# Causal attention in one fp32 product of exponentials and values, instead of two fp16 halves

## What is computed

```python
q = (x @ Wq).reshape(B, S, HEADS, HEAD_DIM).transpose(0, 2, 1, 3)
c_kv = x @ Wkv_down
k = (c_kv @ Wk_up)...        # 16 heads of 32
v = (c_kv @ Wv_up)...
# the last 24 columns of each head of q and k are rotated
scores = jnp.einsum('bhqd,bhkd->bhqk', qf, kf) * scale
scores = jnp.where(causal, -jnp.inf, scores)
weights = jax.nn.softmax(scores, axis=-1)
out = jnp.einsum('bhqk,bhkd->bhqd', weights, v)
```

## Time and profile before

| | |
|---|---|
| median of 3 runs | 1692.59 us (1692.43 to 1700.83) |
| the profiled execution | 1692.4 us, span 1690.6 us |
| PE busy | 1443.2 us (85%), granted clock 0.936 of full |
| DVE busy | 1273.0 us (75%) |
| ACT busy | 903.6 us (53%) |
| POOL busy | 846.8 us (50%) |

### The profile page before, as it was taken

One profiled execution on the slowest core, in us unless ns is written; L12 is line 12 of the kernel. 1 busy time (PEld: TensorE's weight loads), 2 busy tenths in 40 slices (PEclk: granted clock), 3 DMA queues, 4 the chain that ended last, 5 costly groups with the idle time before them and its releaser, 6 DMA issues.

```text
span 1690.6 us, 26867 instructions
## 1 busy us (share of the span) xinstructions
PE 1443.2 (85%) x9924; PEld 869.5 (51%) x9924; DVE 1273.0 (75%) x2115; ACT 903.6 (53%) x1431; POOL 846.8 (50%) x724
## 2 busy tenths in 40 slices
PE   4767787776668988848799999999999999999984
PEld 2345545444544444423356655666566655665553
DVE  4849899899867999975957767767766766766757
ACT  3327566565664544445455565556555565556542
POOL 6418385564352123687644654456454654466421
PEclk9969898989779999968999999999999999999997
DMA  9050010000211010110001000100101100100002
GB/s 282 26 200 2 28 51 2 28 26 27 100 51 50 26 70 32 51 63 13 25 26 38 26 26 29 35 26 26 37 26 31 33 26 26 38 26 26 13 1 100
DMA packets 63105, 74.62 MB, mean 44 GB/s; under 512 B 6912, under 2 KB 40320, under 8 KB 61952
## 3 DMA queue, kind: packets, MB, share of 16 engines
q1 hardware_dynamic: 62400, 68.68, 12.1%
q10 hardware_dynamic: 576, 4.19, 0.6%
HBM read 49.66 MB, written 10.49 MB: 36 GB/s over the span
## 4 chain that ended last, share of the span: by engine, by line
PE 60%; DVE 24%; issue 11%; ACT 3%; POOL 2%; DMA 1%; SPq 0%; DVEq 0%; POOLq 0%; ACTq 0%
PE banks L1103 48%; PE banks L870 6%; DVE nmf L1473 5%; DVE plo L1487 2%; PE banks L935 1%; DVE cat L1456 1%; PE banks L923 1%; DVE top L1599 1%; DVE wk L1595 1%; DVE att L1497 1%; DVE kcT L1463 1%; DMA w_fold<-w_top 1%; DVE attf L1606 1%; PE banks L1058 1%; DVE qcT L1483 1%
## 5 line engine op out<-in xcount | busy, mean ns | idle before, releaser
L1103 PE MATMUL banks<-xc,w 128*128 128x512 f16 x2688 | 591.2, 382 | 17.7 <-ACT banks L1144 15.0
L1103 PEld LDWEIGHTS banks<-xc,w 128*128 128x128 f16 x2688 | 264.2, 99 | 339.2 <-ACT banks L1144 20.2
L1103 PE MATMUL banks<-wd,mid 128*128 128x256 f16 x2688 | 298.1, 273 | 5.4 <-ACT banks L1144 3.1
L1103 PEld LDWEIGHTS banks<-wd,mid 128*128 128x128 f16 x2688 | 263.6, 98 | 40.9 <-ACT banks L1144 3.4
L847 POOL TENSOR_TENSOR mid<-m,mid 128x512 f16<-128x512 f32 x64 | 75.1, 1174 | 318.2 <-ACT mid L1144 318.2
L753 POOL TENSOR_TENSOR plo<-pf,phi 128x896 f16<-128x896 f32 x64 | 133.5, 2088 | 175.3 <-ACT phi L1144 175.2
L1144 ACT ACTIVATE banks<-banks 128x512 f32<-128x512 f32 x192 | 108.7, 579 | 193.0 <-PE banks L1103 193.0
L847 POOL TENSOR_TENSOR mid<-msum,mid 128x512 f16<-128x512 f32 x128 | 186.4, 1475 | 2.6 <-ACT mid L1144 2.6
L1421 DVE SCALAR_TENSOR_TENSOR w<-stage,w 128x512 f16<-128x512 f32 (+1 forms) x56 | 61.5, 1138 | 106.0 <-ACT w L1144 106.0
L1144 ACT ACTIVATE mid<-msum 128x512 f16<-128x512 f32 x128 | 81.2, 635 | 84.1 <-DVE msum L1780 28.1
L1473 DVE TENSOR_REDUCE nmf<-banks 128x1 f32<-128x512 f32 (+3 forms) x256 | 107.3, 480 | 14.9 <-PE banks L937 14.4
(11 more groups left out here) (252 smaller groups left out, 2910.8 us busy)
## 6 DMA issues: line engine op xcount, KB each, us to landing
stage<-w_fold SPq DMA_DIRECT2D x24, 256.0 KB, 3.0
stage<-in_Wg SPq DMA_DIRECT2D x24, 256.0 KB, 3.1
stage<-in_Wu SPq DMA_DIRECT2D x24, 256.0 KB, 3.1
stage<-in_Wd SPq DMA_DIRECT2D x24, 256.0 KB, 2.8
vcat<-vnext SPq DMA_DIRECT2D x8, 528.0 KB, 3.2
x_in<-in_x SPq DMA_DIRECT2D x4, 1024.0 KB, 6.3
x_res<-in_x SPq DMA_DIRECT2D x4, 1024.0 KB, 5.6
c_raw<-in_ctx SPq DMA_DIRECT2D x4, 1024.0 KB, 5.6
```

The lines of the kernel that those rows point to most:

```text
L1103: mm = nc.tensor.matmul(out, l(x, i), r(y, i), start=start and i == 0 and j == 0, stop=stop and i == k - 1 and j == 2, skip_group_check=True)
```

## The change

The exponentials stay as ACT writes them, in float32, and are the stationary operand of one fp32 matmul for each block, against 33 columns of float32 values (32 and the ones). `hi` and `lo` are gone on ACT, POOL and DVE, with `phi` and `plo`; `pf` has four buffers (`PB = 4`). `vcat` and `vnext` hold 33 floats instead of 66 halves, so they have the same bytes and ACT alone writes them (`v` on DVE is gone). `osb` has 33 columns for each block of rows, `comb` loses its addition. The raw weights at the start lie in `pf`. The split of `wqw` stands at other places of the last tables. `A_PE` is unchanged.

```diff
 A_ACT = steps("""
-    xT.0 xT.1 exp.0 xT.2 xT.3 exp.1 hi.0 hi.1 row.0 exp.2 c.0 pv.0 hi.2 row.1 rhi.0 exp.3 row.2 rhi.1 pv.1 hi.3
+    xT.0 xT.1 exp.0 xT.2 xT.3 exp.1 row.0 exp.2 c.0 pv.0 row.1 rhi.0 exp.3 row.2 rhi.1 pv.1 
...
-        vcat = sb(sa, "vcat", [P, H, TT, 66], F16)
-        pf = sb(sa, "pf", [P, 2, TRI])
-        phi = sb(sa, "phi", [P, 2, TRI], F16)
-        plo = sb(sa, "plo", [P, 2, TRI], F16)
-        osb = sb(sa, "osb", [P, 2, G, TT, 65])
+        vcat = sb(sa, "vcat", [P, H, TT, HD + 1])
+        pf = sb(sa, "pf", [P, PB, TRI])
+        osb = sb(sa, "osb", [P, 2, G, TT, HD + 1])
...
                     elif k == "pv":
 
-                        pe.wait_ge(p_lo_pool, own * H + (i + 1 + FREE))
-                        pe.wait_ge(p_lo_dve, own * H + (i + 1 + FREE))
+                        pe.wait_ge(exp_done, own * H + (i + 1 + FREE))
...
-                                for x, w in enumerate((phi, plo)):
-                                    mm = nc.tensor.matmul(out, w[:, i % 2, o:o + P], vcat[:, i, t, 0:65],
-                                                          start=(t == 0 and x == 0), stop=(t == q and x == 1))
+                                mm = nc.tensor.matmul(out, pf[:, i % PB, o:o + P], vcat[:, i, t, :], start=t == 0, stop=t == q)
...
                     elif k == "exp":
                         g = own * H + i
                         act.wait_ge(st_ready, g + (1 + FREE))
-                        act.wait_ge(p_lo_pool, g + (FREE - 1))
-                        act.wait_ge(p_lo_dve, g + (FREE - 1))
-                        nc.scalar.activation(pf[:, i % 2, :], st_ps[:, 0:TRI], ACT.Exp,
+                        act.wait_ge(a_ready["pv"], g + (FREE - PB + 1))
+                        nc.scalar.activation(pf[:, i % PB, :], st_ps[:, 0:TRI], ACT.Exp,
                                              scale=1.0 / (SQ * SQ * math.sqrt(HD))).then_inc(exp_done, 1)
-                    elif k == "hi":
-                        g = own * H + i
-                        act.wait_ge(exp_done, g + (1 + FREE))
-                        act.wait_ge(a_ready["pv"], g + (FREE - 1))
-                        scaled(phi[:, i % 2, :], pf[:, i % 2, :], 1.0).then_inc(p_hi, 1)
...
-                    elif k == "lo":
-                        dve.wait_ge(p_hi, own * H + (i + 1))
-                        tt_(plo[:, i % 2, POOL_COLS:TRI], pf[:, i % 2, POOL_COLS:TRI], phi[:, i % 2, POOL_COLS:TRI],
-                            ALU.subtract).then_inc(p_lo_dve, 1)
...
-                        chain.link(nc.vector.reciprocal(rsum[:, :, :], src[:, :, :, 64]))
-                        chain.link(tt_(o4, src[:, :, :, 0:HD], src[:, :, :, HD:2 * HD], ALU.add))
-                        tt_(o4, o4, rsum[:, :, :].unsqueeze(3).to_broadcast([P, G, TT, HD]), ALU.mult).then_inc(comb_done, 1)
+                        chain.link(nc.vector.reciprocal(rsum[:, :, :], src[:, :, :, HD]))
+                        tt_(o4, src[:, :, :, 0:HD], rsum[:, :, :].unsqueeze(3).to_broadcast([P, G, TT, HD]), ALU.mult).then_inc(comb_done, 1)
...
-            at = last.index(("lo", 14))
+            at = last.index(("comb", 3))
```

More of the change, by code:

```diff
@@ L86 @@
 A_ACT = steps("""
-    xT.0 xT.1 exp.0 xT.2 xT.3 exp.1 hi.0 hi.1 row.0 exp.2 c.0 pv.0 hi.2 row.1 rhi.0 exp.3 row.2 rhi.1 pv.1 hi.3
-    row.3 v.0 exp.4 rhi.2 hi.4 pv.2 row.4 rhi.3 v.1 ln.0 pv.3 v.2 row.5 exp.5 rhi.4 hi.5 row.6 rhi.5 exp.6 pv.4
-    hi.6 row.7 exp.7 rhi.6 pv.5 hi.7 exp.8 pv.6 hi.8 rhi.7 exp.9 pv.7 hi.9 exp.10 pv.8 hi.10 exp.11 hi.11 pv.9
-    exp.12 pv.10 hi.12 exp.13 pv.11 hi.13 exp.14 pv.12 hi.14 exp.15 pv.13 hi.15 v.3 pv.14 pv.15
+    xT.0 xT.1 exp.0 xT.2 xT.3 exp.1 row.0 exp.2 c.0 pv.0 row.1 rhi.0 exp.3 row.2 rhi.1 pv.1
+    row.3 v.0 exp.4 rhi.2 pv.2 row.4 rhi.3 v.1 ln.0 pv.3 v.2 row.5 exp.5 rhi.4 row.6 rhi.5 exp.6 pv.4
+    row.7 exp.7 rhi.6 pv.5 exp.8 pv.6 rhi.7 exp.9 pv.7 exp.10 pv.8 exp.11 pv.9
+    exp.12 pv.10 exp.13 pv.11 exp.14 pv.12 exp.15 pv.13 v.3 pv.14 pv.15
 """)
 A_DVE = steps("""
[L93 to L97, removed]
+    xT.0 xT.1 cat1.0 cat1.1 max.5 xT.2 xT.3 cat1.2 res.0 cat1.3 cat1.4 max.6 cat1.5 res.1 c.0 cat1.6
+    max.7 cat1.7 res.2 mT.1 rlo.0 max.8 rlo.1 max.9 rlo.2 res.3 max.10 rlo.3 max.11
+    ln.0 max.12 rlo.4 mT.2 max.13 cat0.0 rlo.5 cat0.1 max.14 cat0.2 comb.0 cat0.3 cat0.4 max.15
+    rlo.6 cat0.5 rlo.7 cat0.6 cat0.7 mT.3 maxn.0 comb.1 maxn.1 comb.2 maxn.2
+    maxn.3 mTn.0 maxn.4 comb.3
 """)
 A_POOL = steps("""
-    lo.0 rope.0 lo.1 rope.1 lo.2 rope.2 rope.3 lo.3 rope.4 lo.4 rope.5 lo.5 rope.6 lo.6 rope.7 lo.7 lo.8 lo.9
-    lo.10 lo.11 lo.12 lo.13 lo.14 lo.15
+    rope.0 rope.1 rope.2 rope.3 rope.4 rope.5 rope.6 rope.7
 """)
@@ L113 @@
 A_START_DVE = steps("""
-    half.0 half.1 c.0 rlo.0 rlo.1 fold.0 v.0 rlo.2 half.2 fold.1 v.1 rlo.3 half.3 fold.2 v.2 rlo.4 half.4 fold.3 rlo.5
+    half.0 half.1 c.0 rlo.0 rlo.1 fold.0 rlo.2 half.2 fold.1 rlo.3 half.3 fold.2 rlo.4 half.4 fold.3 rlo.5
     half.5 fold.4 fold.5 cat0.0 cat0.1 cat0.2 cat0.3 cat0.4 rlo.6 cat0.5 rlo.7 cat0.6 cat0.7 maxn.0 maxn.1 maxn.2
-    maxn.3 v.3 mTn.0 maxn.4
+    maxn.3 mTn.0 maxn.4
 """)
@@ L318, in decoder @@
         att = sb(sa, "att", [P, TT, D])
[L319 to L323, removed]
+        raw = pf[:, :, :].rearrange("p a n -> p (a n)")
+        raw_wq = raw[:, 0:DT * D].rearrange("p (t n) -> p t n", t=DT)
+        raw_kvd = raw[:, 2048:2048 + DT * LAT].rearrange("p (t n) -> p t n", t=DT)
+        raw_ku = raw[:, 2560:3072]
+        raw_vu = raw[:, 3072:3584]
         w_top = sb(sa, "w_top", [P, 3, 4, 512])
-        w_cat = vcat[:, :, :, :].rearrange("p h t n -> p (h t n)").bitcast(F32)[:, 0:2048].rearrange("p (t n) -> p t n", t=4)
+        w_cat = vcat[:, :, :, :].rearrange("p h t n -> p (h t n)")[:, 0:2048].rearrange("p (t n) -> p t n", t=4)
         w_raw = [w_cat, w_top[:, 0], w_top[:, 1], w_top[:, 2], x_res[:, :, :], att[:, :, :]]
@@ L391, in decoder @@
         a_ready = {k: sem(f"a_{k}_ready") for k in A_PER}
-        a_hi = {k: sem(f"a_{k}_hi") for k in ("xT", "c", "v")}
+        a_hi = {k: sem(f"a_{k}_hi") for k in ("xT", "c")}
         a_drained = {k: sem(f"a_{k}_drained") for k in A_PER}
@@ L696, in _ @@
         def _(pool):
-            for s in [max_done, st_ready, exp_done, p_lo_pool, p_lo_dve, roped, cat_lo, nm_ready, v_moved[0], v_moved[1], comb_done, res_read,
+            for s in [max_done, st_ready, exp_done, roped, cat_lo, nm_ready, v_moved[0], v_moved[1], comb_done, res_read,
                       att_ready, x2_kept] + \
@@ L1191, in heads @@
                             act.wait_ge(comb_done, own * (H // G) + (i // G - 1 + FREE))
-                        scaled(osb[:, i // G % 2, i % G], a_bank(u)[:, 0:TT * 65].rearrange("p (t n) -> p t n", t=TT), 1.0)\
+                        scaled(osb[:, i // G % 2, i % G], a_bank(u)[:, 0:TT * (HD + 1)].rearrange("p (t n) -> p t n", t=TT), 1.0)\
                             .then_inc(a_drained[k], 1)
@@ L1224, in _ @@
             last = own_part(A_ACT, A_NEXT)
-            at = last.index(("hi", 13))
+            at = last.index(("exp", 14))
             heads(last[:at], B - 1, None)
@@ L1484, in heads @@
                             .then_inc(a_drained["mT"], 1)
-                    elif k == "lo":
-                        dve.wait_ge(p_hi, own * H + (i + 1))
-                        tt_(plo[:, i % 2, POOL_COLS:TRI], pf[:, i % 2, POOL_COLS:TRI], phi[:, i % 2, POOL_COLS:TRI],
-                            ALU.subtract).then_inc(p_lo_dve, 1)
                     elif k == "comb":
-                        chain = Chain(dve, comb_step, own * (2 * H // G) + 2 * i)
+                        chain = Chain(dve, comb_step, own * (H // G) + i)
                         dve.wait_ge(comb_done, own * (H // G) + (i + FREE))
@@ L1839 @@
 FREE = 16
-POOL_COLS = 896
+PB = 4
 A_NORM = TT + 4
```

21 lines of the change are left out of this document (6 added, 15 removed).

## The result

| | before | after | ratio, 95% interval |
|---|---|---|---|
| median, first comparison | 1692.5 us (4 runs) | 1723.7 us (4 runs) | 1.018, 1.014 to 1.023 |
| again, beside the later experiments | 1698.9 us (11 runs) | 1721.9 us (6 runs) | 1.014, 1.010 to 1.019 |

The profiled execution took 1732.2 us, the longest of its four. Slower was forecast with a chance of 0.19, and the time lies above the range (1630 to 1702).

A forecast was written before the change was run, and what follows sets the result against it. DVE was taken as the bound of attention (86% busy, PE waiting for it). PE's 312 us busy, 31 of kept waits and 15 for DVE gave 358 against 389, so 1692 would fall to 1661 us; range 1630 to 1702.

The forecast's parts named there:

- PE's busy time: Attention from 96 to 485 us: 276 us today plus 36 for the fp32 products, 312.
- its idle time: PE's waits in attention: 31 us stay (15 on `xT`, 8 at loop turns, 8 for ACT), plus 15 for DVE.
- The price of a product: Products in `pv`: two loads, 110 ns at full clock, 126 at mean clock; 640 cost 81 us against today's 45.
- rival D: Products in `pv`: four loads, 220 ns at full clock; PE pays 117 us, 43 us slower, 1735; chance 0.12.
- The thin place: Product price on PE: slower from 162 ns a matmul at full clock (PE pays 74 us), only half above the forecast price.
- E: Products in `pv`: load and stream in turn, 166 ns, 1695; or stage clock falling to 0.78, 1696; chance 0.13.
- Relief of DVE: Attention: DVE loses 91 us of work and 11 us of slowed operations, from 334.6 to 232 us.
- the sum's 15: PE's waits in attention: of DVE's other 66 us of waits, 15 taken to stay.
- rival C: PE's waits for DVE stay, being latencies of single steps: 45 us instead of 15, 1691, no change; chance 0.10.
- What was costed at nothing: Moved split of `wqw`, smaller copies to `osb`, DMA of the values, the exponentials' new wait: no cost together.

The follow-up runs named there:

- e5: Kernel before with only the product exchanged for the fp32 one (e3), plus values streamed three times a matmul: 1716.8 us, 1.013 to before.
- e2: The change with the 33 columns of values streamed three times in each matmul, copies not read: 1678.6 us, 0.988 to before.
- e4: The change with only the first 64 of each block's 128 stationary columns, half of the rows' attention left out: 1638.2 us, 0.965 to before.
- e10: The change with the values streamed three times a matmul only in the last sequence: 1680.7 us, 0.991 to before.
- e1: The change with one fp16 product in place of the fp32 one, exponentials and values rounded, low halves left out: 1610.2 us, 0.948 to before.
- e6: e2 with three buffers for the exponentials in place of four: 1679.4 us, 0.988 to before.
- e8: Kernel before with exponentials rounded to fp16 in four buffers, one fp16 matmul a block, values still in two halves: 1621.0 us, 0.956 to before.
- e3: Kernel before with only the product exchanged for the fp32 one, high and low halves still made and waited for: 1750.8 us, 1.032 to before.

## Why the prediction was wrong

**Where the 31 us come from.** By medians, one step at a time: the dearer product with its clock kept (e5) costs 18 us against the runs of before beside it (1716.8 - 1698.4); the relief takes off 38 (to e2's 1678.6); the lost clock adds 43 to 45 (to 1721.9 or 1723.7). The sum is 23 to 25 us. It must be, since the steps follow each other from before to the change: this splits the loss and does not check it. The first comparison's 31 us lie higher because its runs of before were faster (1692.5 against 1698 to 1699). And the split depends on the order of the steps, since the relief is worth 27 to 29 us with the low clock and 38 without; e5's clock of the last sequence, 0.87, is also above the 0.81 of before.

Against the forecast's own sum: PE's busy time was put at 312 us in the stage and was 391.8; its idle time was put at 46 and was 28.6 (420.4 - 391.8). The stage took 420 us and not 358, and with 9 us of the start that is the distance from 1661 to the profiled 1732.

**The price of a product** was the term that failed. "I take two loads with a stream of 28 ns under each, 110 ns": two loads with the stream beneath was right in number (1280 for 640 products) and in overlap (e2), and the spacing at half clock is twice that at full, nearly. The size of one load was wrong. The forecast took 55 ns for the columns of the transposes' load, from the loads' durations (140 against 112 ns, 28 for 64 columns). By the same reading the product's load takes 54 ns for 64 columns (192 against 138, e4), and the spacing bears it out: 112 ns for 128 columns, 59 for 64. So a product cost 224 ns. That is rival D's price within 2% (220), and D's charge on PE, 117 us, stands against 116 measured (391.8 - 275.9). That agreement is partly luck: from start to start the products took 53 us before and 176 after, where D had 45 and 162, and PE's other work became 6 us cheaper. Of D's reason, four loads, the trace shows only this much: two load instructions for each product, each as dear as two of the transposes' loads. Whether each goes over the array twice, it cannot tell. The page of the Trainium skill cited for the four passes (FP8 and Floating Point Precision, section TensorE Precision Notes) leaves the loads open. The step that failed is taking a load's price from a transpose: nothing in the trace of before said that it would hold for a product. Why a product's load costs twice as much was not tried.

**The thin place was named.** The forecast put the break-even at 162 ns a product at full clock. It had given D 0.12, and the range did not reach D's time.

**The clock** was weighed in E as a fall of the stage's mean to 0.78 and priced at 35 us. The mean of the stage was 0.83, and it fell in one place, the last sequence, from 0.81 to 0.55, where it cost about 40 us (e2, e10). The argument against it, that PE is asked for more work in less time, is what failed: PE was busier, and the array streamed less. The clock fell where PE hardly idled. Whether idling explains the 0.81 of before, no run shows.

**Relief of DVE.** DVE's busy time was forecast at 232 us and came to 229.9. L1498's successor has a mean of 692 ns, as said, and L1456's has 846 where 1000 was taken. PE's waits for DVE were forecast at 30 us in all; besides the 15.1 on `xT`, no row of PE's waits for DVE is over 2 us. A dear product hides such waits, so the fair case is e4, near the price that was forecast. There PE waited 15.2 us on `xT` and some 10 for DVE's other steps, in six rows of which this is the largest:

```profile
PE banks L926 <- DVE nmf L1452: 3.9, 5, 1.3
```

So the sum's 15 was on the high side and rival C is out. e4, at 118 ns a product, came to 1638 where the same sum gives 1661. Most of the distance is PE's own term (295 us and not 312), the rest its idle time (35 and not 46). With the product cheaper than before the waits come back: in e1 they are 44 us for DVE beside `xT`, 16.3 of them for the maxima.

**What was costed at nothing.** The four buffers (three do as well, e6) and everything behind the stage were rightly left out. The start was not forecast to differ either; its 9 us in the profile are the clock of that execution, not the change. The moved split of `wqw` and the smaller copies were not tried by themselves.

## What to carry to other kernels

Price an fp32 product by its weight loads: with few moving columns they set the pace here, and a load's price in a transpose was not that in a product. When work goes from DVE to PE, look for the clock of the new work too: here a stretch of loads with short streams ran at half clock while the profile called PE 94% busy. Repeated moving columns that fit under the load cost nothing there and gave back 43 to 45 us. A single fp16 product (e8), where rounded exponentials are good enough, takes some 100 us less than the change and 77 less than the kernel before.

## What the hardware did that I had not expected

- Loads of 128 fp32 columns set a spacing of 112 ns in a product at full clock, those of 64 columns 59 (e4). The loads' durations differ by 54 ns for these 64 columns, and by 28 in transposes, where the load lies under the stream and no spacing shows it.
- The stream of 33, 66 or 99 columns under these loads leaves the spacing at 112 ns, but moves the granted clock of the last sequence from 0.55 to 0.96 and 0.98. PE's busy share was higher at the low clock (94% against 86%).
- DVE's product over 128x512 floats in `comb` takes 691 to 693 ns 16 times of 16 after the change, against a mean of 986 and a longest of 2264 before. The three long ones of before all lie beside a subtraction of POOL, but one product that lies wholly beside one took 691, and in e3, where POOL still subtracts, all 16 products take 691 to 693 and only the addition before them reaches 2102. So POOL as the cause is not shown:

```profile
L1471 DVE TENSOR_TENSOR att<-osb,rsum x16: 691/692/693, 173.9 to 525.9; 128x512 f32<-128x512 f32 x16
```

- The first 96 to 105 us, nearly the same code in all of these kernels, have a granted clock of 0.93 in some executions and 0.76 to 0.90 in others. The profile's column reads 1.00 for the first 20 us of the kernel before, although its transposes there stand 213 to 215 ns apart, the spacing at half clock: in the first microseconds the distance between matmuls says more than the column. Why the clock differs was not tried.
